# An order of work changed in the opening of two mixture-of-experts phases, and three edits in the recurrent phase between them

## The reference, cut to what matters

```
x = x + 0.5 * ffn(layernorm(x))      # ffn phase 1: 8 experts, top 2 of 8, and a shared expert
x = x + mamba2(layernorm(x))         # middle phase, the two sequences one after the other
x = x + 0.5 * ffn(layernorm(x))      # ffn phase 2: the same weights as phase 1

def ffn(x):
    logits = x @ router_w.T
    scores, top_idx = top_k(logits, 2)
    moe = sum over the two picked experts of score * (silu(x @ wg[e]) * (x @ wu[e])) @ wd[e]
    return moe + (silu(x @ sg_w + sg_b) * (x @ su_w + su_b)) @ sd_w + sd_b
```

## Time and profile before

| | us |
|---|---|
| median of 3 runs (2335.07 to 2339.71) | 2339.08 |
| the profiled execution | 2342.91 |
| its span, first to last instruction | 2340.1 |
| mean granted TensorE clock of it | 0.964 of full |
| first expert phase | 0 to 370 |
| middle phase | 370 to 1972 |
| second expert phase | 1972 to 2340 |

### The profile page before, as it was taken

How to read it: one execution, slowest core, us unless ns; L and a number is a source line. 1 busy time by engine, 2 the same in 40 slices (tenths; PEclk the granted TensorE clock), 3 DMA queues, 4 the chain that set the end, 5 groups by cost and what they waited for, 6 DMA issues and landing times. The chain is left out here.

```text
span 2340.1 us, 42981 instructions
## 1 busy us (share of the span) xinstructions
PE 2154.7 (92%) x11718; PEld 1744.9 (75%) x11718; DVE 1478.8 (63%) x2954; ACT 1433.0 (61%) x2961; POOL 1375.0 (59%) x1242
## 2 busy tenths in 40 slices
PE   5799996699999999999988999999999996689996
PEld 3577774588888888888766888888888884467775
DVE  6422247567777776777877777777777777732225
ACT  5133322687778778777657877778778773423331
POOL 2876351466667666666516666667666663486632
PEclk8899997899999999999998999999999998899998
DMA  9655461434333343433214334333333421365545
GB/s 344 243 164 166 128 173 49 99 83 126 101 95 107 108 107 85 129 95 94 66 48 124 99 90 116 104 102 102 113 102 86 122 79 33 139 217 166 164 141 166
DMA packets 204903, 285.31 MB, mean 122 GB/s; under 512 B 16288, under 2 KB 148458, under 8 KB 204816
## 3 DMA queue, kind: packets, MB, share of 16 engines
q1 hardware_dynamic: 185936, 219.18, 32.0%
q0 software_dynamic: 18880, 65.02, 9.2%
HBM read 225.43 MB, written 58.72 MB: 121 GB/s over the span
## 5 line engine op out<-in xcount | busy, mean ns | idle before, releaser
L2016 PE MATMUL mamba_p_proj<-mamba_xt_lo,mamba_in_hi 128*128 128x512 f32 x1056 | 457.2, 433 | 1.7 <-DVE mamba_bc L1690 1.2
L1690 DVE SCALAR_TENSOR_TENSOR mamba_xs<-mamba_p_proj,mamba_taps,mamba_xs 128x511 f32<-128x511 f32 (+2 forms) x384 | 285.9, 745 | 260.5 <-ACT mamba_xs L1439 251.6
L2018 PE MATMUL mamba_p_proj<-mamba_xt_hi,mamba_in_lo 128*128 128x512 f32 x1056 | 416.5, 394 | 0.0
L2017 PE MATMUL mamba_p_proj<-mamba_xt_hi,mamba_in_hi 128*128 128x512 f32 x1056 | 414.3, 392 | 0.0
L1312 POOL TENSOR_TENSOR mamba_xend<-mamba_xdt,mamba_to_end_g 128x512 f32<-128x512 f32 x128 | 134.1, 1047 | 350.7 <-DVE mamba_xdt L1750 293.3
L1318 POOL TENSOR_TENSOR mamba_mix<-mamba_mix,mamba_scores 128x512 f32<-128x512 f32 x256 | 325.7, 1293 | 15.0 <-ACT mamba_mix L1505 15.0
L1501 ACT ACTIVATE mamba_mix<-mamba_cum_l,mamba_cum_g 128x128 f32<-128x128 f32 x1024 | 324.8, 389 | 4.6 <-PE mamba_p_y L2124 1.0
L660 DVE TENSOR_TENSOR ffn_h<-ffn_p_gu,ffn_sil 128x256 f32<-128x256 f32 x110 | 46.9, 426 | 330.1 <-ACT ffn_sil L545 309.8
L545 ACT ACTIVATE ffn_sil<-ffn_p_gu 128x256 f32<-128x256 f32 x110 | 42.3, 385 | 324.7 <-PE ffn_p_gu L905 242.2
L2018 PEld LDWEIGHTS mamba_p_proj<-mamba_xt_hi,mamba_in_lo 128*128 128x128 f32 x1056 | 199.7, 189 | 46.6
L2016 PEld LDWEIGHTS mamba_p_proj<-mamba_xt_lo,mamba_in_hi 128*128 128x128 f32 x1056 | 200.9, 190 | 40.9 <-DVE mamba_bc L1690 2.0
(11 more groups left out here) (338 smaller groups left out, 5123.3 us busy)
## 6 DMA issues: line engine op xcount, KB each, us to landing
mamba_cum_l<-mamba_cum_rows SPq DMA_DIRECT2D x128, 512.0 KB, 5.2
mamba_rise<-mamba_exp_rows SPq DMA_DIRECT2D x256, 128.0 KB, 3.4
ffn_xs<-slots_in SPq DMA_DIRECT2D x78, 256.0 KB, 2.7
slots_out<-ffn_y SPq DMA_DIRECT2D x78, 256.0 KB
mamba_raw_x<-in_t SPq DMA_DIRECT2D x34, 512.0 KB, 4.5
mamba_raw_z<-in_t SPq DMA_DIRECT2D x32, 512.0 KB, 5.3
mamba_raw_out<-out_t SPq DMA_DIRECT2D x32, 512.0 KB, 4.7
slots_out<-ffn_xs SPq DMA_DIRECT2D x1, 9984.0 KB
```

Of the source, the lines that this page charges most:

```text
L1690: dve.scalar_tensor_tensor(dst[:, i:BLK], p_proj[:, ct, 0:BLK - i], tap[:, 0, j:j + 1], dst[:, i:BLK], ALU.mult, ALU.add).then_inc(s_conv, 1)
L2016: pe.matmul(bank, in_hi[:, piece, kk, :], xt_lo[:, kk, c], start=(kk == 0), stop=False)
L2017: pe.matmul(bank, in_hi[:, piece, kk, :], xt_hi[:, kk, c], start=False, stop=False)
L2018: last = pe.matmul(bank, in_lo[:, piece, kk, :], xt_hi[:, kk, c], start=False, stop=(kk == KT - 1))
```

## The change

It edits the opening of both expert phases and three places in the middle phase.

- PE computes a block's scores one tile sooner (at tile 5, 9, 13 instead of 6, 10, 14) and turns them back one tile sooner. The counts of the first half come after tile 12 instead of 14. The last block's scores now stand before job 0, and only their turning back behind it.
- DVE ranks the first half after tile 10 (before: 11) and places it after tile 12 (before: 13). The low parts of the shared expert's weights move from tile 7 to behind the places at tile 12 (`low_in`), and from tile 9 to 14 (`low_out` and the biases). ACT's rounding of them moves from tiles 3, 5 and 7 to 11, 12 and 13.
- The rounding of expert 1's weights moves from ahead of job 0 to behind jobs 2 and 3 on ACT; the low parts on DVE go behind `turns` and behind job 3.
- POOL sends the first four tiles before it issues the loads of expert 1's weights, and the loads of expert 2's weights come behind all scatters instead of between the two halves.
- The row statistics of the first eight tiles (the first sequence) for the second expert phase are computed in the middle phase: DVE does one or two tiles at a time in its last slot and tail, with the root on ACT and the scale on DVE there too. The second expert phase starts with them known (`ready` = 8) and computes only blocks 2 and 3.
- `exp_t` moves from `xdt` to `rise`; DVE's wait for the store goes.
- `load_in` for group 1 is issued right behind the first `load_rise`, ahead of the two `load_cum` of block 1. In the loop the order of the queue is as before, written as decays first and then the next group's `load_in`.

```diff
@@ ffn_phase, gpsimd
-            def scatter(half):
+            def scatter(half, tiles):
                 pool.wait_ge(s_route, half + 1)
-                for t in range(half * HALF, (half + 1) * HALF):
+                for t in tiles:
...
+            scatter(0, range(HALF // 2))
             load_gate(1)
             load_up(1)
             load_out(1)
-            scatter(0)
+            scatter(0, range(HALF // 2, HALF))
+            scatter(1, range(HALF, T))
             load_gate(2)
             load_up(2)
             load_out(2)
-            scatter(1)
@@ ffn_phase, scalar
-            roots(0)
+            if not known:
+                roots(0)
...
-                    if (t + AHEAD) % TPB == 0:
+                    if (t + AHEAD) % TPB == 0 and not known:
                         roots((t + AHEAD) // TPB)
                     rows(t + AHEAD)
                 high_l(t)
-                if t > TPB and t % TPB == 2:
+                if known and t % TPB == TPB - 1 and t // TPB + known < NB:
+                    roots(t // TPB + known)
+                if t > TPB and t % TPB == 1:
                     log_row(t // TPB - 1)
-                if t == 3:
+                if t == HALF + 2:
+                    low_logits(0)
+                if t == HALF + 3:
                     round_in(0)
-                if t == 5:
+                if t == HALF + 4:
                     round_out(0)
-                if t == 7:
+                if t == HALF + 5:
                     act.wait_ge(s_const, 6)
                     round_biases()
-                if t == HALF + 3:
-                    low_logits(0)
-            round_in(1)
             log_row(T // TPB - 1)
             low_logits(1)
-            round_out(1)
             for g in range(JOBS):
                 tick(g)
+                if g == 2:
+                    round_in(1)
+                if g == 3:
+                    round_out(1)
@@ ffn_phase, vector
-            stats(0)
-            scale(0)
+            if not known:
+                stats(0)
+                scale(0)
             for t in range(T):
-                if t % TPB == 0 and t // TPB + 1 < NB:
-                    stats(t // TPB + 1)
+                b = t // TPB + max(known, 1)
+                if known and t % TPB == 0 and known < b <= NB:
+                    scale(b - 1)
+                if t % TPB == 0 and b < NB:
+                    stats(b)
                 low_l(t)
-                if t % TPB == 0 and t // TPB + 1 < NB:
-                    scale(t // TPB + 1)
-                if t == 7:
+                if not known and t % TPB == 0 and b < NB:
+                    scale(b)
+                if t == HALF + 2:
+                    rank_first(0)
+                    rank_second(0)
+                if t == HALF + 4:
+                    places(0)
                     low_in(0)
-                if t == HALF + 1:
+                if t == HALF + 6:
                     low_out(0)
                     low_biases()
-                if t == HALF + 3:
-                    rank_first(0)
-                    rank_second(0)
-                if t == HALF + 5:
-                    places(0)
-            low_in(1)
             rank_first(1)
             rank_second(1)
             tick(0)
             places(1)
-            low_out(1)
             tick(1)
             tick(2)
             turns()
+            low_in(1)
             tick(3)
+            low_out(1)
             order_pairs()
@@ ffn_phase, tensor
-                if t > TPB and t % TPB == 2:
+                if t > TPB and t % TPB == 1:
                     score(t // TPB - 1)
-                if t == HALF + 6:
+                if t == HALF + 4:
                     pe.wait_ge(s_const, 16)
                     count(0)
-                if t > TPB and t % TPB == 3:
+                if t > TPB and t % TPB == 2:
                     log_columns(t // TPB - 1)
+            score(T // TPB - 1)
             pe.wait_ge(s_bias, 6)
             tick(0)
-            score(T // TPB - 1)
             log_columns(T // TPB - 1)
@@ mamba_phase
-        exp_t = xdt[0:HEADS, :, :, :].rearrange("p c h d -> p (c h d)")
+        exp_t = rise[0:HEADS, :, :, :].rearrange("p j c l -> p (j c l)")
@@ mamba_phase, sync
                 for j in range(2):
                     load_rise(k, 0, 0, j, first=True)
+                load_in(sx + 2, GC + X0, sz + 6, GC + Z0)
                 for j in range(2):
                     load_cum(k, 0, 1, j)
-                with sp.Fori(1, G) as gi:
-                    load_in(gi + (sx + 1), gi * GC + X0, gi * 4 + (sz + 2), gi * GC + Z0)
+
+                def decays(gi):
...
+                with sp.Fori(1, G - 1) as gi:
+                    decays(gi)
+                    load_in(gi + (sx + 2), gi * GC + (GC + X0), gi * 4 + (sz + 6), gi * GC + (GC + Z0))
+                decays(G - 1)
@@ mamba_phase, scalar
+            act.wait_ge(s_next_var, 1)
+            act.activation(norm["root"][:, NEXT], norm["var"][:, NEXT], ACT.Sqrt).then_inc(s_next_root, 1)
             rms_root(batches - 1)
@@ mamba_phase, vector
+            def next_norm(*tiles):
+                for t in tiles:
+                    dve.bn_stats(lns.stat[:, t % 2, :], x[:, t, :]).then_inc(s_next, 1)
+                    dve.wait_ge(s_next, 2 * t + 1)
+                    dve.bn_aggr(norm["moments"][:, t, :], lns.stat[:, t % 2, :]).then_inc(s_next, 1)
...
                 carry_of(0)
                 next_state(0)
+                if last and not more:
+                    next_norm(0, 1)
...
                 carry_of(1)
                 next_state(1)
+                if last and not more:
+                    next_norm(2, 3)
...
-                dve.wait_ge(s_stored, (k + 1) * 32)
                 times_dt(k, 0, 0, 0, first=True)
...
-            for t in range(TPB):
+            next_norm(4, 5)
+            accumulate(batches * UNITS - 1, NB - 1, 0)
+            next_norm(6)
+            accumulate(batches * UNITS - 1, NB - 1, 1)
+            next_norm(7)
+            dve.wait_ge(s_next, 2 * (batches - 1) * T)
+            dve.tensor_scalar(norm["var"][:, NEXT], norm["moments"][:, NEXT, 1], LN_EPS, None,
+                              ALU.add).then_inc(s_next_var, 1)
+            for t in range(2, TPB):
                 accumulate(batches * UNITS - 1, NB - 1, t)
+            dve.wait_ge(s_next_root, 1)
+            refine_rsqrt(dve, link(dve, s_next_fin), norm["rstd"][:, NEXT], norm["root"][:, NEXT], norm["var"][:, NEXT],
+                         norm["tmp"][:, NEXT])
+            dve.scalar_tensor_tensor(norm["shift"][:, NEXT], norm["moments"][:, NEXT, 0], -1.0, norm["rstd"][:, NEXT],
+                                     ALU.mult, ALU.mult)
             mean_square(batches - 1)
```

## The result

The changed kernel took 2355.57 us (median of 11 runs, 2344.77 to 2364.78) where the kernel before took 2339.08 (11 runs): a ratio of 1.0066, 95% interval 1.0046 to 1.0085. The forecast was 2307 us. The profiled execution took 2355.45 with a span of 2353.7.

What follows compares the result with a forecast made beforehand. PE, full in steady stretches, idles in the openings, where the chain from slots to routed load decides. 4.9 + 16.4 + 11.1 - 0.2 = 32.2 us off the profiled 2342.9 gives 2310.7, less 3.8 to the median: 2307, bounds 2297 to 2320.

Steps and rivals of the forecast that it cites:

- POOL's chain: Expert openings: 32 scatters keep their 44.0 us behind the slots; last ends at 92.6 and 2044.7 us.
- The second phase's slots: Second expert phase's opening: slots at 2000.8 instead of 2017.1 us, 16.4 us sooner, bounds 10 and 18.
- the forecast's lump of 3.4 us for a score: Second expert phase: PE's score of block 1, 2.05 us in the trace, taken as 3.4 at mean clock 0.71.
- The middle phase: Opening 11.1 us sooner, ACT's wait for `raw_x` giving way to one for `cum_l`; tail 0.2 us later.
- The first expert phase: Opening: slots at about 48.5 instead of 53.4 us, 4.9 us sooner, bounds 2.4 and 6.4.
- 2.9 us of slack: First expert phase: `places(1)` at 68.4, POOL reaching the second half's slots at about 71.3 us.
- the moves whose price is hidden: Expert openings: expert 1's later splitting and expert 2's later weight loads are covered, costing nothing.
- the late silus: Expert openings: ACT stands 29.3 and 28.6 us on "remote", read as tied to the scatters' stream.
- B: Rival: late silus keep their length, fall partly on the second half's ranking, taking back 4 us per phase: 2315; chance 0.13.
- D: Rival: late silus follow ACT's instruction count, so the stall lies ahead of `places(1)` with POOL idle: 2359; chance 0.05.
- the chain from the slots to the load: Expert openings: slots, 32 scatters, landing, load set when PE fills up; first loads near 95.8 and 2047.5 us.
- More than 20 us are in hand: First expert phase: expert 2's weights, asked for at 92.6, are in time for its first tile near 135 us.

Runs made afterwards that it cites:

- set B: Two groups of runs in which the kernel before took 2312.6 and 2313.1 us; none of their profiles has late silus.
- set A: The first comparison and three more groups of runs, in which the kernel before took 2338 to 2340 us; every profile has late silus.
- m_middle: Changed kernel with both expert phases' openings as before, middle phase's edits and statistics kept: 2316.94 us, ratio 0.9914 in set A; 2289.72, 0.9905 in set B.
- b_tail: Changed kernel with DVE's low parts of biases and output weights moved later, and PE turning the last scores back ahead of job 0: 2330.34 us, ratio 0.9973, set A.
- k_tail: b_tail run again: 2329.76 us, ratio 0.9954, set A.
- k_both: b_tail with `order_pairs` right behind `turns` on DVE, ahead of expert 1's low parts: 2329.59 us, ratio 0.9959, set A.
- o_one: Changed kernel with expert 1's split back ahead of job 0 on ACT and around the second half's ranking on DVE: 2330.74 us, ratio 0.9966, set A.
- h_one: o_one run again: 2331.3 us, ratio 0.9973, set A.
- s_score: Changed kernel with PE running job 0 ahead of the last block's scores again: 2356.3 us, ratio 1.0086, set A.
- h_score: s_score run again: 2357.73 us, ratio 1.0075, set A.
- f_free: Changed kernel with the DVE cast that the clearing waits for moved right behind the second half's places: 2361.03 us, ratio 1.0103, set A.
- h_pad: Changed kernel with 64 small transposes more on PE at the head of each expert phase: 2366.98 us, ratio 1.0119, set A.
- k_after: The changed kernel run again: 2357.02 us, ratio 1.007, set A.
- d_pairs: Changed kernel with `order_pairs` right behind `turns` on DVE, ahead of expert 1's low parts: 2288.52 us, ratio 0.9892, again 2289.5, 0.9904, both set B.

## Why the prediction was wrong

**POOL's chain, right.** First scatter at 48.17, last scatter ending 92.4, in the second phase 70.3 us after its start; in set B 94.8 and 71.6. The second phase's slots came 18.6 us sooner from its start (44.43 to 25.77, set B), where 16.4 were forecast; of that, the forecast's lump of 3.4 us for a score was too long, as the 2.05 us of the earlier trace rows were at a granted clock of 1.00, and 2.05 / 0.71 is 2.9.

**The middle phase, right.** Forecast 11.1 less 0.2; measured 9.3 in set A, 10.6 in set B. And by the mechanism: in set B ACT's wait for `raw_x` is gone and a new one for `cum_l` stands in its place (ACT, changed kernel):

```profile
427.58 0.63 ACT L1495 ACTIVATE mamba_in_hi<-mamba_raw_x 128x512 fp32r<-128x512 f32 x1 [0.16 <-DMA mamba_raw_x<-in_t]
...
430.45 1.28 ACT L1519 ACTIVATE mamba_mix<-mamba_cum_l,mamba_cum_g 128x128 f32<-128x128 f32 x4 [2.24 <-DMA mamba_cum_l<-mamba_cum_rows]
```

**The first expert phase, wrong even where nothing is late.** In set B it gained 0.1 us instead of 4.9; the second gained 15.1 of 16.4, so that with the middle phase's 10.6 the gain was 25.8 of 32.2 (the span was 25.2 shorter). The step that failed is "tick 0 on DVE and the last scores stand in its way: 2.9 us of slack": I put `places(1)` at 68.4, and it came at 70.9, since the low parts that I had moved away from the first ranking (2.6 us of output weights and biases, at tile 14) stood ahead of the last tile, PE waited 6.0 us for that, and then ran job 0 before it turned the scores back. POOL didn't wait for it; its chain took 46.6 us from first start to last end instead of 44.2. But PE lost at the front what it gained at the load: its waits in the first 130 us, without those for ACT's rows, sum to 24.6 us before and 25.2 after. By job 8 it was even 2.2 us ahead (ACT's silu at 108.6 against 110.8), at a granted clock of 1.00 from 100 to 130 us where the kernel before had 0.85; jobs 15 to 46 gave 2.1 of that back, for a reason that I didn't find. I had said of the moved steps what engine they leave, and not whom they now stand ahead of.

**The cost put at nothing, wrong by some 38 us in set A.** Late instructions cost the kernel before 17.1 and 13.8 us in the two expert phases (set A less set B), the changed one 34.4 and 34.5. All of the growth is there by job 8: from 3.0 and 2.8 us to 22.1 and 22.1. The failed step is the one on "the moves whose price is hidden" and the late silus: I named them, "tied to the scatters' stream", put their price in as unchanged, and had rivals in which they cost more only with the second half's ranking (B and D). Two things were wrong with it.

First, the wait for the routed tile that the change removes was what hid the late instructions. It took up 14.0 and 12.8 us of them before, and 3.3 and 1.5 after (job 7 less job 8 in the table above): 10.7 and 11.3 us of the growth. The prediction took the chain from the slots to the load as what sets when PE fills up, but in set A PE didn't wait for that load before: the 6.4 us of the earlier trace rows were a wait behind the late silu.

Second, 8.4 and 8.0 us are new lateness, and it comes between jobs 5 and 7. The stall fell on PE's job 4 and on what stands ahead of `turns`, which before had run from 75.9 to 82.2 and came at 88.1 now. `order_pairs`, behind it and behind expert 1's late split, then ran into POOL's splitting of expert 2, took 12.2 and 12.3 us instead of 4.1, and PE stood 7.62 us behind it. The prediction never asked where `turns`, the clearing and `order_pairs` would be, since they were covered by the scatters; the cover now ended 5 us sooner, and what it covered began 12 us later. "More than 20 us are in hand" looked at expert 2's first tile alone, not at what else DVE does while POOL splits.

Rival D gave 2359, near the 2355.6, but by luck: it put the stall ahead of `places(1)`, and there POOL waited 0.5 us.

What the runs show is this much: in set A the kernels whose `turns` ended by 87 in the first phase (m_middle 78.8, b_tail 78.1, k_tail and k_both 80.2, o_one 85.6, h_one 86.8) are faster than the kernel before, and those where it ended at 89 to 101 (changed, s_score, h_score, f_free, h_pad) are slower; none in between. That `turns` itself is the cause isn't shown: two of the edits that make it early also change what DVE and PE have in their queues in the stretch from 83 to 97. f_free, which frees only the clearing from it, gains nothing, and of two traces of the changed kernel in set A the one with the earlier end (89.6, k_after, beside 96.1) has the longer phase (389.1 beside 387.0). What `order_pairs` took divides the kernels in the same way: 4.1 to 5.5 us in both phases of the faster ones, 7.7 to 16.5 in the slower ones, where it meets POOL's splitting (16.5 in k_after). This has a wait of PE behind it in the trace, but it wasn't tested alone: d_pairs, which would, ran in set B only.

**Open.** What makes instructions late in set A isn't known; with number 7 in both sets it is rather something that changes with time than the chip, if that number is the same chip. That it is the supply of instructions is an argument, from the steps of 0.70 us on two engines and from the page's DMA view, which has a kind "instruction". The queues from 70 to 100 us, changed kernel, set A (all that there are), then set B:

```profile
q0 software_dynamic: 1537, 5.02, 45.9%
q1 hardware_dynamic: 432, 0.79, 6.8%
```

```profile
q0 software_dynamic: 1853, 6.16, 54.9%
q1 hardware_dynamic: 1152, 2.10, 18.9%
q8 instruction: 1, 0.02, 0.3%
q14 instruction: 1, 0.01, 0.1%
```

In these 30 us each of the seven profiles of set A that are no slower than the kernel before has two or three such packets, and of the six of the slower kernels five have none. It doesn't settle the matter: a packet can be late because the engine that it is for is, no row says which engine that is, and h_pad has one (q8) and is as late. The scatters' part wasn't tried, since I could not take half of them away without leaving memory unwritten. But ten of the 13 profiles of set A have a late silu of 11 us or more near the end of the second phase too, where POOL sends no scatters but gathers, also indirect DMAs, as in the kernel before:

```profile
2308.77 0.38 ACT L545 ACTIVATE ffn_sil<-ffn_p_gu 128x256 f32<-128x256 f32 x1 [11.56 <-remote]
```

The middle phase, where POOL sends none, is the same in both sets to 0.7 us. So as far as these traces go, the lateness is found beside POOL's indirect DMAs, in set A only. The Trainium skill, "Runtime: NRT & Kernel Launch", section "Instruction fetch mechanics", has each sequencer fetch its instructions ahead by a DMA queue of its own and calls the cost of crossing from one block to the next mostly hidden. Set B agrees (no such gap in any of its seven traces); in set A, if the reading is right, it is not hidden while POOL's indirect DMAs run.

## What to carry to other kernels

A step that is moved out of one chain stands ahead of another: for each, write down what is queued behind it at its new place, and follow every job that was covered (here `turns`, the clearing, `order_pairs`) until it is covered again. An idle time for which the trace has no cause is no constant of the kernel; ask what it would cost if it doubled, and give that a real chance. Ask also which wait hides it now: a change that takes that wait away pays for it in full. And run the kernel before beside every candidate: d_pairs would have passed for a gain of 2.8% over the changed kernel, and was none.

## What the runs showed of the hardware

The same program took 2339 and 2313 us in two sets of runs, each steady within about 0.5%, at the same granted clock in the steady stretches (1.00 and 0.99 from 500 to 1200 us); the difference lies in the two expert phases (17.1 and 13.8 us; the middle phase differs by 0.7). Only 3.0 and 2.8 us of it are there by job 8; 8.8 and 7.9 come in the last three jobs of a phase, beside POOL's gathers.

DVE's small instructions stretch beside POOL's. `order_pairs` took 12.2 us instead of 4.1; DVE and POOL of the changed kernel in set A:

```profile
102.79 1.87 DVE L795 TENSOR_TENSOR ffn_ordered<-ffn_slot_f 128x16 int32<-128x16 f32 x1
...
104.91 2.23 DVE L797 TENSOR_TENSOR ffn_lower<-ffn_slot_f 128x16 f32<-128x16 f32 x1
```

```profile
102.73 1.90 POOL L386 TENSOR_TENSOR ffn_in_hi<-ffn_raw_in,ffn_one 128x1024 fp32r<-128x1024 f32 x1 [0.98 <-DMA ffn_raw_in<-wg]
104.71 2.39 POOL L388 TENSOR_TENSOR ffn_in_lo<-ffn_raw_in,ffn_in_hi 128x1024 fp32r<-128x1024 f32 x1
```

DVE's two end at 104.66 and 107.14, POOL's at 104.63 and 107.10; the same instructions take 0.17 us while POOL sends scatters (set B). The Trainium skill, "SBUF — State Buffer", section "SBUF: two separate sides", says that DVE and GpSimd share a pair of ports, that whichever starts first has it for a whole instruction, and that the other, if it is a DVE instruction with two inputs in SBUF beside one of GpSimd that reads SBUF, waits; the trace agrees, with 1.7 and 2.1 us of waiting inside instructions of 0.17.
